# A metaformer kernel: the first convolution's line sums, column maxima and group-norm statistics are computed on other engines

## What is computed

```python
g = x.reshape(b * GROUPS, cg, h, w)
def branch(ph, pw):
    hw = conv1x1(jnp.concatenate([ph, pw], axis=2))
    ah, aw = (hw[:, :, :h], hw[:, :, h:])
    gated = g * sigmoid(ah)[..., None] * sigmoid(aw)[:, :, None, :]
    return gnorm(gated)                      # mean and variance of each channel
x1 = branch(g.mean(axis=3), g.mean(axis=2))  # the average branch
y1 = branch(g.max(axis=3), g.max(axis=2))    # the maximum branch
x12 = softmax(x1.mean(axis=(2, 3)))
y12 = softmax(y1.max(axis=(2, 3)))
weights = einsum(x12, y1) + einsum(y12, x1)
out = g * sigmoid(weights)
```

## Time and profile before

| | |
|---|---|
| median of 3 runs | 1347.95 us (1347.94 to 1348.74) |
| span of the profiled execution | 1347.4 us |
| TensorE busy | 978.5 us (73%) |
| VectorE busy | 867.6 us (64%) |
| ScalarE busy | 586.7 us (44%) |
| GpSimd busy | 444.0 us (33%) |

### The profile page before, as it was taken

One profiled execution on the slowest core, in us unless ns is written; L12 is line 12 of the kernel. 1 busy time (PEld: TensorE's weight loads), 2 busy tenths in 40 slices (PEclk: granted clock), 3 DMA queues, 4 the chain that ended last, 5 costly groups with the idle time before them and its releaser, 6 DMA issues.

```text
span 1347.4 us, 24878 instructions
## 1 busy us (share of the span) xinstructions
PE 978.5 (73%) x7761; PEld 830.6 (62%) x7761; DVE 867.6 (64%) x1854; ACT 586.7 (44%) x1055; POOL 444.0 (33%) x486
## 2 busy tenths in 40 slices
PE   5210667556699999999502669349999999999943
PEld 4100457426588888888401559128888888888832
DVE  6999689897454455555599885844555555545545
ACT  5200223275465555555524434455444444444422
POOL 1385000000055555555342540013444444444420
PEclk8655795558799999999855875559999999999965
DMA  7000007707522333332384302011111111111148
GB/s 227 1 0 0 0 1 249 250 0 241 180 96 92 125 125 125 125 121 67 124 265 161 109 32 94 16 47 35 49 49 47 51 51 48 47 47 47 47 145 260
DMA packets 88924, 127.80 MB, mean 95 GB/s; under 512 B 7920, under 2 KB 71864, under 8 KB 88760
## 3 DMA queue, kind: packets, MB, share of 16 engines
q1 hardware_dynamic: 70536, 84.34, 19.2%
q0 software_dynamic: 14000, 38.82, 8.8%
q10 hardware_dynamic: 4352, 4.20, 1.0%
HBM read 96.39 MB, written 30.93 MB: 94 GB/s over the span
## 4 chain that ended last, share of the span: by engine, by line
PE 58%; DVE 19%; issue 9%; DMA 7%; ACT 4%; DVEq 1%; POOL 1%; ACTq 0%; SPq 0%; POOLq 0%
PE bank L695 24%; PE bank L713 19%; PE bank L619 4%; PE bank L536 3%; PE bank L681 2%; DMA rows_y<-region,put_now 2%; DMA wreg<-rows_y 2%; DVE region L1031 2%; DVE tok L1372 2%; PE bank L755 2%; ACT xt L860 2%; DVE xt L1043 2%; DVE tok L1377 2%; PE bank L591 1%; DMA wreg<-in_L_ffn_w_dram 1%
## 5 line engine op out<-in xcount | busy, mean ns | idle before, releaser
L695 PE MATMUL bank<-region,wreg 128*128 128x256 f16 x3360 | 383.2, 275 | 11.0 <-issue 11.0
L695 PEld LDWEIGHTS bank<-region,wreg 128*128 128x128 f16 x3360 | 328.0, 99 | 55.0 <-issue 11.4
L713 PE MATMUL bank<-wreg,region 128*128 128x256 f16 x2520 | 298.2, 273 | 1.1 <-DVE region L1346 0.7
L713 PEld LDWEIGHTS bank<-wreg,region 128*128 128x128 f16 x2520 | 242.3, 98 | 31.0 <-DVE region L1346 2.7
L889 ACT ACTIVATE region<-bank,b_t,fac 128x256 f32<-128x256 f32 x280 | 142.9, 560 | 87.4 <-PE bank L695 84.0
L471 POOL DMA_INDIRECT rows_y<-region,put_now x140 | 150.7, 1076 | 87.8 <-issue 45.9
L432 POOL DMA_INDIRECT region<-rows_x,fetch_now x144 | 141.9, 986 | 92.9 <-POOL fetch_now L477 62.8
L1342 DVE SCALAR_TENSOR_TENSOR region<-bank,fac,region 128x256 f32<-128x256 f32 x140 | 61.3, 479 | 148.1 <-PE bank L695 80.5
L536 PE MATMUL bank<-ident,xn 128*128 128x128 f32 x256 | 57.0, 385 | 114.1 <-DVE xn L1002 106.6
L866 ACT ACTIVATE region<-bank 128x1024 f16<-128x1024 f16 x72 | 73.7, 1024 | 135.3 <-PE bank L681 135.1
L536 PEld LDWEIGHTS bank<-ident,xn 128*128 128x128 f32 x256 | 46.2, 209 | 123.0 <-DVE xn L1002 112.8
(11 more groups left out here) (240 smaller groups left out, 1365.5 us busy)
## 6 DMA issues: line engine op xcount, KB each, us to landing
wreg<-in_L_ffn_w_dram SPq DMA_DIRECT2D x48, 512.0 KB, 5.9
wreg<-in_L_ffn_w_dram SPq DMA_DIRECT2D x16, 1024.0 KB
wreg<-rows_y SPq DMA_DIRECT2D x48, 256.0 KB, 3.7
region<-in_L_ffn_w_dram SPq DMA_DIRECT2D x12, 1024.0 KB, 7.4
rows_x<-region SPq DMA_DIRECT2D x16, 512.0 KB, 3.1
wreg<-in_x_dram SPq DMA_DIRECT2D x4, 1024.0 KB, 9.7
out_dram<-xt ACTq DMA_DIRECT2D x16, 256.0 KB, 3.6
region<-rows_x,fetch_now POOLq DMA_INDIRECT x144
```

Source lines behind the costliest of these rows:

```text
L695: last = pe.matmul(to, w[:, e, k, ws_, c * P:(c + 1) * P], x_cols[:, k, xs_, :], start=(k == 0 and ws_ + xs_ == 0), stop=(k == KC - 1 and ...
L713: last = pe.matmul(yb[:, r * C:(r + 1) * C], lhs[:, c, r * P:(r + 1) * P], w[:, e, c, ws_, :], start=first, stop=end, skip_group_check=True)
```

## The change

1. **Line sums by TensorE.** GpSimd and VectorE build a pattern `line_pat` of zeros and ones, 128 places by 32 columns for each of the two tiles of an image: 16 columns say in which row a place lies, 16 in which column. In the normalising loop TensorE, after the two images' transposes, multiplies each of their eight 128x128 pieces of `xn` (as weights) with the pattern (`sum_lines`), adding up in `zb[k]`. `xn[:, j]` may be overwritten only when `lines_summed[j]` is there, so VectorE's `norm` waits for that too. ScalarE copies both banks to `line[:, 0]` at the end. VectorE's four sum reductions go.
2. **Column maxima by a tree.** The strided maximum reduction of each half becomes four `tensor_tensor` maxima, of 16 rows to 8, 4, 2 and 1, in the order of a `chain`, through `gated[:, 1, k]`.
3. **Statistics of the average branch on ScalarE.** For each half 16 copies with an accumulated sum, three small scalings to means, and 16 squares of the difference with an accumulated sum, after `gated_by_pool`; the 32 `bn_stats` of `r` = 0 go from VectorE. `deviations(4, ...)` waits for them (`gn_sums`).
4. **Gating shared anew.** GpSimd still does both gatings of (0, 0) and (0, 1), but of (1, 1) only the rows; VectorE does the columns of (1, 1).
5. Semaphores: five `var_ready` become one with counts, five `sd_ready` too.

```diff
@@ gpsimd, constants @@
-        CONSTS = 17
+        CONSTS = 19
...
+            by_row = line_pat[:, :, 0:HW]
+            nc.gpsimd.affine_select(out=by_row, in_=ones[:, 0:2 * HW].rearrange("p (h l) -> p h l", h=2), compare_op=ALU.is_ge,
+                                    fill=0.0, base=0, pattern=[[P, 2], [-HW, HW]], channel_multiplier=1).then_inc(consts, 1)
...
+            nc.gpsimd.affine_select(out=by_row, in_=by_row, compare_op=ALU.is_ge, fill=0.0, base=HW - 1,
+                                    pattern=[[-P, 2], [HW, HW]], channel_multiplier=-1).then_inc(consts, 1)
@@ gpsimd, gating @@
-                gate_by_rows(nc.gpsimd, r, k).then_inc(pool_mid, 1)
-                pool.wait_ge(pool_mid, n + 1)
-                gate_by_columns(nc.gpsimd, r, k).then_inc(gated_by_pool, 1)
+                by_rows = gate_by_rows(nc.gpsimd, r, k)
+                if r == 0:
+                    by_rows.then_inc(pool_mid, 1)
+                    pool.wait_ge(pool_mid, n + 1)
+                    gate_by_columns(nc.gpsimd, r, k).then_inc(gated_by_pool, 1)
+                else:
+                    by_rows.then_inc(gated_by_pool, 1)
@@ tensor @@
+            def sum_lines(i, j):
+                for k in range(KC):
+                    for h in range(UT):
+                        u = 2 * i + j
+                        last = pe.matmul(zb[k][:, bass.ds(u * 2 * HW, 2 * HW)], xn[:, j, h, k * P:(k + 1) * P], line_pat[:, h, :],
+                                         start=(h == 0), stop=(h == 1))
+                last.then_inc(lines_summed[j], 1)
+
+            pe.wait_ge(pattern_ready, 1)
+            pe.wait_ge(nat_copied, 3)
             def turn_normed(i):
                 for j in range(2):
                     norm_turn(0, i, j)
+                for j in range(2):
+                    sum_lines(i, j)
...
-                    pe.wait_ge(lines_ready, 2 * (r * KC + k) + 2)
+                    if r == 0:
+                        pe.wait_ge(sums_ready, k + 1)
+                    else:
+                        pe.wait_ge(lines_ready, 2 * k + 2)
                     pe.matmul(zb[2 * r + k][:], conv_bd[:], line[:, r, k].rearrange("p b l -> p (b l)"),
@@ scalar @@
+            for j in range(2):
+                act.wait_ge(lines_summed[j], HB)
+            for k in range(KC):
+                act.activation(line[:, 0, k].rearrange("p b l -> p (b l)"), zb[k][:], ACT.Copy).then_inc(sums_ready, 1)
             act.wait_ge(small_ready, 1)
... (the four sigmoids)
+            taken = 0
+            for k in range(KC):
+                act.wait_ge(gated_by_pool, k + 1)
+                at = slice(k * NB, (k + 1) * NB)
+                for b in range(NB):
+                    n = k * NB + b
+                    free(act, gn_sums, taken - 5)
+                    act.activation(stats_out[:, b % 6], gated[:, 0, k, b * L:(b + 1) * L], ACT.Copy, accum_out=sum_gn[:, n:n + 1]
+                                   ).then_inc(gn_sums, 1)
+                    taken += 1
+                act.wait_ge(gn_sums, taken)
+                act.activation(neg_mean_gn[:, at], sum_gn[:, at], ACT.Copy, scale=-1.0 / L).then_inc(gn_sums, 1)
+                for half in (1, 4):
+                    act.activation(st_gn[:, at, half], sum_gn[:, at], ACT.Copy, scale=1.0 / L).then_inc(gn_sums, 1)
+                taken += 3
+                act.wait_ge(gn_sums, taken)
+                for b in range(NB):
+                    n = k * NB + b
+                    free(act, gn_sums, taken - 5)
+                    act.activation(stats_out[:, b % 6], gated[:, 0, k, b * L:(b + 1) * L], ACT.Square, bias=neg_mean_gn[:, n:n + 1],
+                                   accum_out=st_gn[:, n, 2:3]).then_inc(gn_sums, 1)
+                    taken += 1
+                act.wait_ge(gn_sums, taken)
             deviation(4)
@@ vector @@
             def norm(s, i, j):
+                if s == 0:
+                    free(dve, lines_summed[j], i)
                 free(dve, xn_turned[j], HB * s + i)
...
-            for r, op in enumerate((ALU.add, ALU.max)):
-                for k in range(KC):
-                    v = g[:, k, :].rearrange("p (b h w) -> p b h w", b=NB, h=HW)
-                    dve.tensor_reduce(line[:, r, k, :, 0:HW], v, AX.X, op).then_inc(lines_ready, 1)
-                    dve.tensor_reduce(line[:, r, k, :, HW:2 * HW], v.rearrange("p b h w -> p b w h"), AX.X, op).then_inc(lines_ready, 1)
+            dve.memset(st_gn[:, 0:KC * NB, 5], 0.0).then_inc(gn_stats, 1)
+            for k in range(KC):
+                v = g[:, k, :].rearrange("p (b h w) -> p b h w", b=NB, h=HW)
+                dve.tensor_reduce(line[:, 1, k, :, 0:HW], v, AX.X, ALU.max).then_inc(lines_ready, 1)
+                to = gated[:, 1, k, :].rearrange("p (b h w) -> p b h w", b=NB, h=HW)
+                chain(dve.tensor_tensor(to[:, :, 0:8], v[:, :, 0:8], v[:, :, 8:16], ALU.max))
+                chain(dve.tensor_tensor(to[:, :, 0:4], to[:, :, 0:4], to[:, :, 4:8], ALU.max))
+                chain(dve.tensor_tensor(to[:, :, 0:2], to[:, :, 0:2], to[:, :, 2:4], ALU.max))
+                dve.tensor_tensor(line[:, 1, k, :, HW:2 * HW], to[:, :, 0], to[:, :, 1], ALU.max).then_inc(lines_ready, 1)
...
-            dve.wait_ge(gated_by_pool, 1)
-            channel_stats(0, 0)
...
-            dve.wait_ge(gated_by_pool, 2)
-            channel_stats(0, 1)
             dve.wait_ge(gated_mid, 2)
             channel_stats(1, 0)
             maxima(0)
             dve.wait_ge(gated_by_pool, 3)
+            gate_by_columns(dve, 1, 1).then_inc(gated_mid, 1)
+            dve.wait_ge(gated_mid, 3)
             channel_stats(1, 1)
```

## The result

The changed kernel takes 1367.07 us (median of 4 runs, 1366.98 to 1367.91), the kernel before beside it 1348.35 us. The ratio is 1.0136, with a 95% interval of 1.0121 to 1.0150: slower by 18.7 us. 1371.6 had been forecast, 23.7 us slower.

The account below looks back on a forecast made before the run. It took VectorE's chain and the normalising loop's ring, 24.8 to 134.95 us, as the bound. The delay, 157.3 - 134.95 + 1.3 = 23.7, gave 1347.4 + 23.7 + 0.55 = 1371.6 us; range 1355 to 1380.

Parts of the forecast that it names:

- TensorE's clock in the loop: Normalising loop: granted clock stays at 0.50 (1.2 GHz) throughout, so VectorE begins on `g` 27.1 us later.
- rival 1: Normalising loop: TensorE's clock rises as before, rounds take 3.4 us, statistics end at 142.5: +8.9, 1356.8 us; chance 0.16.
- A round of 5.8 us: Normalising loop: 5.37 us of transposes and products plus 0.4 to 0.5 of handover to VectorE, per round.
- Products hide behind their weights: Line sums on TensorE: 32 columns cost no more than 8, as the next weight load runs beside; 0.22 us per record.
- Maxima by turns with GpSimd: Tree on VectorE: its steps alternate with GpSimd's whole multiplications; 38.0 us from 76.0, lines complete at 114.0.
- the straight line: Tree step sizes, interpolated between 256 and 4096 elements: 2.29, 1.23, 0.69 and 0.43 us, together 4.64.
- To the statistics: From complete lines at 114.0 through sigmoid, signs, gatings, statistics and maxima: end at 157.3 us, against 134.95.
- ScalarE's statistics are hidden: Average branch: 64 activations at 0.42 us plus 3, done at 147, before VectorE's 157.3; they add nothing.
- Rival 2: ScalarE's statistics set the end, at 0.7 us per activation with accumulation: end at 164.7, +31, 1379 us; chance 0.10.
- Table load in the chain: Square root: its 1.28 us table load now waits for `var_ready`, adding 1.3 us.
- Rival 3: Tree is not held up by GpSimd: 1352.5 us at the low clock, 1336 with the clock up; chance 0.06.
- The sum: Whole kernel: 157.3 - 134.95 + 1.3 = 23.7 us slower, 1371.6 us.

Follow-up runs that it names:

- e2: Changed kernel with the line-sum pattern 128 columns wide instead of 32, same result, loop's eight rounds written out: 1359.66 us, ratio 1.0068.
- e9: e7 with columns of (1,1) on VectorE and GpSimd's rows of (1,1) waiting for VectorE's columns of (1,0): 1338.30 us, ratio 0.9890.
- e1: Changed kernel with the tree of maxima taken back to the strided reduction: 1360.74 us, ratio 1.0099.
- e6: Changed kernel with one wait more, GpSimd's gating starting only when all maxima are complete: 1374.54 us, ratio 1.0150.
- e7: Kernel before with only average-branch statistics on ScalarE and count semaphores, without ScalarE's last wait for those statistics: 1340.69 us, ratio 0.9906.

## Why the prediction was right, point by point

- **TensorE's clock in the loop** stays at 1.2 GHz: right, and in e2, with wider products in a loop written out, rival 1 came true: deviations at 141.71, where it had 142.5. By what the Trainium skill says (TensorE: Matmul & The Clock Gate, "What's actually happening": activity releases the throttle) I had given rival 1 its chance. The changed kernel's trace doesn't agree with it as I had read it: 38.81 us busy of 40.20 at 0.50.
- **A round of 5.8 us** was too long: 5.42. This is the term that was mis-sized. I added 0.4 to 0.5 for the handover to the router's 5.37, but the 16 narrow records take 3.28 us here (32.33 to 35.61) against 3.43 there (803.61 to 807.04), and the transposes with the handover 2.14 against 1.94 without one. So the handover costs 0.2, not 0.4 to 0.5, and the rest is the records' pace; why that is quicker here no run shows. Seven rounds make 2.7 us. Against that the loop began at 25.18, 0.3 later than I had it. VectorE began on `g` at 65.94, not 68.1, and GpSimd at 73.44, not 76.0.
- **Products hide behind their weights** (32 columns): right. A record takes 0.205 us (3.28 / 16), no more than the router's with 8 columns (0.214).
- **Maxima by turns with GpSimd**: from GpSimd's start to complete lines 37.0 us, forecast 38.0. The sizes from the straight line, 2.29, 1.23, 0.69 and 0.43, were measured as 2.28, 1.22, 0.69 and 0.42. The statement that reductions and `bn_stats` keep their length beside GpSimd is right, but the 5.32 named for it stands where GpSimd is idle (88.92 to 94.89); e9 shows it, with 16 in 5.32 us beside GpSimd's 7.18.
- **To the statistics**: from complete lines to `deviations` 43.1, forecast 43.3. Right in the sum. The step that says signs cost 0.6 held only because GpSimd was idle there (108.2 to 114.1); in e1 and e6 it did not. The prediction's turns have GpSimd idle there too, but it did not see that the step hung on it.
- **ScalarE's statistics are hidden**: right, 0.40 and 0.49 against 0.42, with 10.4 us to spare before `deviations`. Rival 2 needed 0.6.
- **Table load in the chain**: right, 1.28; e7 takes it out again.
- **Rival 3**, that the tree is not held up: out. But its arithmetic is wrong too. It lets the end come 19 us earlier at the low clock (1352.5 for 1371.6). In e1 the maxima do not wait and lines are complete 22 us earlier, with GpSimd starting as before, and deviations come only 8.3 us earlier; in e6 nothing in the tree waits, GpSimd starts later, and the end comes later. I had let the tree's waits vanish and not asked what waits for GpSimd behind them.
- **The sum**: 23.7 forecast, 19.9 at the first product of the mixing loop, 17.8 in the span, 18.7 between the medians. Of the 3.8 between the first two, the loop's rounds, through GpSimd's start, are 2.6, the turns 1.0 and the statistics 0.2; the 2.1 between mixing loop and span lie in stages that the change doesn't touch. What moves these by some us from kernel to kernel I did not test. They shift when the block before them ends at another time, and TensorE's clock, which rises and falls there, is the suspect only.

## What to carry to other kernels

Count VectorE and GpSimd's multiplications as one engine for what was seen to wait here: operations on two tensors in SBUF, even of one element, and `tensor_scalar` of 256 elements. Reductions and `bn_stats` did not wait; of other operations these runs say nothing. Then look at the order in which they take turns: a short step between two long instructions of the other costs up to their whole length, and a wait that keeps the long ones away from each other (e9) need not cost anything. Work moved off the busiest engine gains where the receiving engine idles under it (ScalarE's statistics) and loses where it lengthens a ring that runs before it (TensorE's sums). And where narrow products on TensorE go with a clock that stays down, it is worth trying them padded with zeros, as in e2.

## What the runs showed of the hardware

- A `tensor_scalar` of 256 float32 elements in SBUF waits for GpSimd's multiplication like an operation on two tensors (14.17 us for two of 0.31 in e1, 16.17 in e6); one of a single element doesn't (0.15).
- The granted clock rose to 1.00 between 29.2 and 33.4 us of e2, with 128-column products in a loop written out; TensorE was busy 8.01 of 8.60 us there (24.8 to 33.4). In the changed kernel, with 32-column ones, it stayed at 0.50 with TensorE busy 38.81 of 40.20 us. Width and loop form were not tried apart.
- ScalarE's accumulated sum costs next to nothing in a stream: the copies of 256 elements follow each other at 0.40 us, with the reading instruction of 0.19 overlapping the next one. In the kernel before, two activations of 256 elements without it (L884, which writes float16) take 0.81 us together.
